# Graph network layer: features rotated and turned a batch ahead, radial units regrouped, axes summed on VectorE

## The reference

```
x = _layernorm(x + _L0_gnn_ref(x, src, dst), axis=-1)
x = _layernorm(x + _L1_gnn_ref(x, edge_weight, edge_attr_3, edge_index, w1, b1, w2, b2), axis=-1)
...
R = jax.nn.relu(abs_distances[:, None] @ w1 + b1) @ w2 + b2
Y = spherical_harmonics(rel_vec)
Fj = features[src]
...
            acc = acc + _NORM[i] * jnp.einsum('euv,ef,evi,ofi->euo', Rb[..., k], Yf, Fb, C)
...
out = out.at[dst].add(msg)
```

## Time and profile before

| | us |
|---|---|
| median of 3 runs (lowest, highest) | 3802.49 (3800.13, 3803.61) |
| the profiled execution | 3798.03 |
| its span | 3796.3 |
| TensorE busy | 3310.6 (87%) |
| GpSimd busy | 2786.3 (73%) |
| VectorE busy | 2762.8 (73%) |
| ScalarE busy | 2061.5 (54%) |

### The profile page before, as it was taken

The page is one execution under the profiler, slowest core; times in us unless marked ns, Lnnn a source line. Parts: engine busy times, 40 slices in busy tenths (PEclk is TensorE's granted clock), DMA queues, the critical chain, the costliest instruction groups (busy, mean ns, idle before and its releaser), DMA issues.

```text
span 3796.3 us, 58108 instructions
## 1 busy us (share of the span) xinstructions
PE 3310.6 (87%) x17312; PEld 1902.1 (50%) x17312; DVE 2762.8 (73%) x3470; ACT 2061.5 (54%) x2391; POOL 2786.3 (73%) x2915
## 2 busy tenths in 40 slices
PE   4999999999999883399999999999999999999963
PEld 3898889898989783222323232333323232323232
DVE  5787877787878785467777777777777777777765
ACT  4777777776777660145454545454554545454520
POOL 6777777777777776677777777777777777777746
PEclk9999999999999995599999999999999999999975
DMA  4122222222122211122222222222222222222211
GB/s 100 39 57 41 52 43 43 50 44 54 40 55 43 50 48 29 39 57 53 62 55 59 55 59 55 59 58 56 62 52 62 55 59 54 59 55 59 57 28 26
DMA packets 188428, 197.65 MB, mean 52 GB/s; under 512 B 60241, under 2 KB 149427, under 8 KB 188085
## 3 DMA queue, kind: packets, MB, share of 16 engines
q1 hardware_dynamic: 95508, 149.13, 13.7%
q0 software_dynamic: 92832, 47.72, 9.7%
HBM read 134.02 MB, written 62.59 MB: 52 GB/s over the span
## 4 chain that ended last, share of the span: by engine, by line
PE 70%; ACT 12%; DVE 5%; POOL 5%; issue 5%; DMA 1%; SPq 0%; ACTq 0%; DVEq 0%; POOLq 0%
PE ps_r L940 19%; PE ps_r L990 17%; PE ps_m L1027 10%; PE ps_m L940 10%; PE ps_r L1018 8%; ACT prod_room L822 8%; POOL ngot L667 4%; DVE unit L1645 3%; PE ps_m L1037 2%; PE ps_r L1002 2%; ACT f_across L829 2%; PE ps_r L924 1%; ACT hot_s L739 1%; PE ps_m L1043 1%; ACT hot_s L742 1%
## 5 line engine op out<-in xcount | busy, mean ns | idle before, releaser
L688 POOL DMA_INDIRECT got<-x_d,idx x1564 | 1506.2, 963 | 530.6 <-issue 504.7
L822 ACT ACTIVATE prod_room<-ps_r,bias_col 128x1024 f32<-128x1024 f32 x392 | 435.9, 1112 | 780.0 <-PE ps_r L990 531.9
L940 PE MATMUL ps_r<-x_hi,hot_s 128*128 128x448 f32 x1974 | 741.6, 376 | 41.7 <-ACT hot_s L742 41.7
L1645 DVE TENSOR_TENSOR x_room<-radial_more,ps_r 128x1024 f32<-128x1024 f32 x392 | 475.0, 1212 | 384.0 <-PE ps_r L1018 252.3
L990 PE MATMUL ps_r<-hid,wc 64*128 64x512 f32 (+1 forms) x2352 | 669.8, 646 | 81.2 <-ACT prod_room L822 72.9
L940 PE MATMUL ps_r<-x_lo,hot_s 128*128 128x448 f32 x1974 | 733.0, 371 | 0.0
L739 ACT ACTIVATE hot_s<-rows,minus_row 128x512 fp32r<-128x512 f16 (+1 forms) x658 | 449.0, 764 | 244.0 <-PE ps_m L940 206.2
L1018 PE MATMUL ps_r<-ft,repeat 32*128 32x512 f32 (+1 forms) x2352 | 553.4, 639 | 1.1 <-ACT ft L848 0.6
L1645 DVE TENSOR_TENSOR unit<-prod_room,ps_r 128x1024 f32<-128x1024 f32 x392 | 451.1, 1213 | 106.9 <-PE ps_r L1018 102.0
L940 PEld LDWEIGHTS ps_r<-x_hi,hot_s 128*128 128x128 f32 x1974 | 378.3, 192 | 75.5 <-issue 43.0
L990 PEld LDWEIGHTS ps_r<-hid,wc 64*128 64x128 f32 x2352 | 178.8, 186 | 448.8 <-ACT prod_room L822 255.3
(11 more groups left out here) (203 smaller groups left out, 4438.4 us busy)
## 6 DMA issues: line engine op xcount, KB each, us to landing
hid<-weight_t SPq DMA_DIRECT2D x196, 256.0 KB
run_d<-runs_t SPq DMA_DIRECT2D x194, 256.0 KB
got<-x_d,idx POOLq DMA_INDIRECT x1564
rows<-code_d SPq DMA_DIRECT2D x47, 160.0 KB
frame_d<-x_sb SPq DMA_DIRECT2D x7, 1008.0 KB, 4.5
frame<-frame_d SPq DMA_DIRECT2D x98, 72.0 KB
frame_b<-frame_d SPq DMA_DIRECT2D x98, 72.0 KB
rows<-code_d SPq DMA_DIRECT2D x47, 128.0 KB
```

Source lines behind the costliest of these rows:

```text
L688: pool.indirect_dma_start(got[k][:, t, :], None, x1_d, bass.IndirectOffsetOnAxis(ap=idx[k][:, t:t + 1], axis=0)).then_inc(got2_landed[k], 16)
L822: act.activation(radial_s[u][:, :, 0:w], radial_slot[:, :, 0:w], ACT.Identity, bias=bias_col[:, c:c + 1]).then_inc(radial_copied, 1)
L940: mm = pe.matmul(found[BANK_OF[k][g]], hot_s[k][:, a, g, :], part[:, a * LN * D:(a + 1) * LN * D], start=(a == 0 and n == 0), stop=(a == B ...
L1645: dve.tensor_tensor(product[q][h][:, :, 0:w], radial_s[u][:, :, 0:w], spread_slot[(k + s_ + 1) % 2][:, :, 0:w], ALU.mult).then_inc(multipl ...
```

## The change

Nothing of what is computed changes, and GpSimd's and SyncE's code stays as it is. In the message stage:

- Batch b + 1 is rotated in the body of batch b, between its multiplies 5 and 6, and turned, copied and given its index copy there. Transposed features get a bank of their own role (`turned_p`, the messages' bank), and `ft` two buffers, so the six spreads have both slots to themselves.
- Three radial units are made in the batch that uses them (3 to 5), three a batch ahead (0 to 2). The rectified weights (`relu`) are made one batch ahead rather than two.
- `add_axes` goes from TensorE. VectorE copies the scalars into `terms2` and adds the three axes with two instructions; `terms2` lies in SBUF now, so carry and scan read it there.

Some SBUF buffers of the input stage and the message stage share space differently; the order of the input stage doesn't change.

```diff
-STEPS = {"layer0": 8, "layer1": 16, "frames": 21}
+STEPS = {"layer0": 8, "layer1": 20, "frames": 21}
...
-ft = sb("ft", [P, QUAD * P])
+ft = [sb(f"ft{k}", [P, QUAD * P]) for k in range(2)]
...
-scalars_s = f_across[1][:, :, :, :, :].rearrange("p t a b v -> p (t a b v)")[:, 0:T * MUL].rearrange("p (t u) -> p t u", u=MUL)
+terms2 = f_across[1][:, :, :, :, :].rearrange("p t a b v -> p (t a b v)").rearrange("p (o t) -> p o t", t=T)
...
-terms2 = ps_m[:, 0, :].rearrange("p (o t) -> p o t", t=T)
+turned_p = ps_m[:, 0, :]
...
+def copy_turned(b, k, w=QUAD * P):
+
+    act.wait_ge(turned, b + 1)
+    if not isinstance(b, int) or b > 1:
+        act.wait_ge(spread_ready, UNITS * (b - 1))
+    act.copy(ft[k][:, 0:w], turned_p[:, 0:w]).then_inc(ft_ready, 1)
...
             masks2(b - 1, 1 - k)
+        copy_radial(b, 3, w)
+        copy_radial(b, 4, w)
         if not final:
-            later = TL // QUAD * P if last else QUAD * P
-            for u in range(4):
-                copy_radial(b + 1, u, later)
+            relu(1 - k, i + k + 1)
+        copy_radial(b, 5, w)
         if not first:
             carry_and_turn(b - 1, 1 - k)
-        if not last:
-            relu(k, i + 2)
         if not final:
-            copy_radial(b + 1, 4, later)
+            copy_radial(b + 1, 0, later)
+            copy_radial(b + 1, 1, later)
+            copy_scalars(b + 1, 1 - k, i + k, n)
+            if not last:
+                act.copy(idx[1 - k][:, :], src_all[:, bass.ds((b + 3) * T, T)]).then_inc(idx_ready, 1)
+            copy_turned(b + 1, 1 - k, later)
+            copy_radial(b + 1, 2, later)
...
-    if not isinstance(b, int) or b > 0:
-        pe.wait_ge(multiplied, len(PRODUCTS) * b - 1)
+    if not isinstance(b, int) or b > 1:
+        pe.wait_ge(back_ready, b - 1)
     for j in range(w // P):
-        mm = pe.transpose(spread_slot[k][:, 0, j * P:(j + 1) * P],
+        mm = pe.transpose(turned_p[:, j * P:(j + 1) * P],
...
-    slot = spread_slot[(k + s + 1) % 2]
+    slot = spread_slot[s % 2]
...
-        if not isinstance(b, int) or b > 0:
-            pe.wait_ge(multiplied, len(PRODUCTS) * b)
+    if s < 2 and (not isinstance(b, int) or b > 0):
+        pe.wait_ge(multiplied, len(PRODUCTS) * (b - 1) + s + 7)
...
-    if not isinstance(b, int) or b > 0:
-        pe.wait_ge(scanned, BATCHES + b)
+    pe.wait_ge(ft_ready, b + 1)
...
-def add_axes(b, n=T):
-    pe.wait_ge(back_ready, b + 1)
-    for a in range(3):
-        pe.matmul(terms2[:, MUL:D, :].rearrange("p (u i) t -> p t i u", i=3)[:, 0:n], ident[:, :],
-                  back[:, a, 0:n], start=(a == 0), stop=(a == 2), skip_group_check=True)
-    pe.matmul(terms2[:, 0:MUL, :].rearrange("p u t -> p t u")[:, 0:n], ident[:, :],
-              scalars_s[:, 0:n, :], start=False, stop=True, skip_group_check=True).then_inc(axes_summed, 1)
...
+        spread_features(b, k, 0, w)
         if not first:
             sum_products(b - 1, 3)
+        spread_features(b, k, 1, w)
+        if not first:
             turn_messages(b - 1)
-        turn_features(b, k, w)
+        radial(b, k, 3, w)
+        spread_features(b, k, 2, w)
+        radial(b, k, 4, w)
+        sum_products(b, 0, w)
+        radial(b, k, 5, w)
+        spread_features(b, k, 3, w)
+        sum_products(b, 1, w)
         if not final:
             radial(b + 1, 1 - k, 0, later)
-        spread_features(b, k, 0, w)
-        spread_features(b, k, 1, w)
-        if not first:
-            add_axes(b - 1)
+        spread_features(b, k, 4, w)
         if not final:
             radial(b + 1, 1 - k, 1, later)
-        spread_features(b, k, 2, w)
-        sum_products(b, 0, w)
-        sum_products(b, 1, w)
+        spread_features(b, k, 5, w)
         if not final:
             radial(b + 1, 1 - k, 2, later)
-        spread_features(b, k, 3, w)
-        if not final:
-            radial(b + 1, 1 - k, 3, later)
-        spread_features(b, k, 4, w)
-        if not final:
-            radial(b + 1, 1 - k, 4, later)
-        spread_features(b, k, 5, w)
+            turn_features(b + 1, 1 - k, later)
         sum_products(b, 2, w)
-        if not final:
-            radial(b + 1, 1 - k, 5, later)
...
-    s.mark(dve.tensor_copy(scalars_s[:, 0:n, :], messages[:, 0:n, 0:MUL]))
+    s.mark(dve.tensor_copy(terms2[:, 0:MUL, :].rearrange("p u t -> p t u")[:, 0:n], messages[:, 0:n, 0:MUL]))
...
     ins.then_inc(back_ready, 1)
+    s.settle()
+    s.mark(dve.tensor_tensor(back[:, 0, 0:n], back[:, 0, 0:n], back[:, 1, 0:n], ALU.add))
+    s.settle()
+    dve.wait_ge(back_ready, b + 1)
+    s.mark(dve.tensor_tensor(terms2[:, MUL:D, :].rearrange("p (u i) t -> p t i u", i=3)[:, 0:n],
+                             back[:, 0, 0:n], back[:, 2, 0:n], ALU.add))
...
-    dve.wait_ge(axes_summed, b + 1)
     dve.wait_ge(masks2_ready, b + 1)
+    s.settle()
...
+def rotate(b, k, rounds, n=T):
+
...
+        multiply(b, k, 0, w)
+        multiply(b, k, 1, w)
+        if begun:
             turn_back(b - 1, 1 - k)
-        for m in range(4):
-            multiply(b, k, m, w)
-        if not (first and k == 0):
+        multiply(b, k, 2, w)
+        multiply(b, k, 3, w)
+        multiply(b, k, 4, w)
+        if begun:
             scan2(b - 1, 1 - k)
-        for m in range(4, len(PRODUCTS)):
-            multiply(b, k, m, w)
-
+        multiply(b, k, 5, w)
+        if not final:
+            rotate(b + 1, 1 - k, i + k, TL if last else T)
+        multiply(b, k, 6, w)
+        multiply(b, k, 7, w)
+
+rotate(0, 0, 0)
```

More of the change, by code:

```diff
@@ L834, in layer1 @@
                     first, final = isinstance(b, int) and b == 0, last and k == 1
-                    n = TL if final else T
-                    w = TL // QUAD * P if final else QUAD * P
+                    n = TL if last else T
+                    w = (TL if final else T) // QUAD * P
+                    later = n // QUAD * P
                     if not first:
                         copy_summed(b - 1)
-                    act.wait_ge(got2_landed[k], 16 * (T * i + n))
-                    if not isinstance(b, int) or b > 1:
-                        act.wait_ge(turned, b - 1)
@@ L862, in _ @@
             act.wait_ge(loaded_net, 96)
             relu(0, 1)
-            relu(1, 1)
             act.wait_ge(bias_ready, 1)
-            for u in range(UNITS - 1):
+            for u in range(3):
                 copy_radial(0, u)
+            copy_scalars(0, 0, 0, T)
+            act.copy(idx[0][:, :], src_all[:, 2 * T:3 * T]).then_inc(idx_ready, 1)
+            copy_turned(0, 0)
             layer1(0)
@@ L1087, in _ @@
             mm.then_inc(bias_turned, 1)
-            for u in range(UNITS):
+            for u in range(3):
                 radial(0, 0, u)
@@ L1091, in _ @@
             pe.wait_ge(spreads_made, 1)
+            turn_features(0, 0)
             layer1(0)
@@ L1644, in multiply @@
                     dve.wait_ge(summed, BLOCKS * (b - 1) + q + 1)
-                dve.tensor_tensor(product[q][h][:, :, 0:w], radial_s[u][:, :, 0:w], spread_slot[(k + s_ + 1) % 2][:, :, 0:w],
+                dve.tensor_tensor(product[q][h][:, :, 0:w], radial_s[u][:, :, 0:w], spread_slot[s_ % 2][:, :, 0:w],
                                   ALU.mult).then_inc(multiplied, 1)
+            def rotate(b, k, rounds, n=T):
+                dve.wait_ge(got2_landed[k], 16 * (T * rounds + n))
+                dve.wait_ge(frame_loaded[k], 16 * (rounds + 1))
+                f1 = got[k][:, 0:n, MUL:D].rearrange("p t (v c) -> p t v c", c=3)
+                for c in range(3):
+                    s.mark(dve.tensor_tensor(part[:, c, 0:n], spread(f1[:, :, :, c], 2, 3),
+                                             spread(frame[k][:, 0:n, c, :], 3, MUL), ALU.mult))
+                s.settle()
+                s.mark(dve.tensor_tensor(part[:, 0, 0:n], part[:, 0, 0:n], part[:, 1, 0:n], ALU.add))
+                s.settle()
+                if not isinstance(b, int) or b > 1:
+                    dve.wait_ge(turned, b - 1)
+                dve.tensor_tensor(turned_in[k][:, 0:n, MUL:D], part[:, 0, 0:n].rearrange("p t i v -> p t (i v)"),
+                                  part[:, 2, 0:n].rearrange("p t i v -> p t (i v)"), ALU.add).then_inc(rotated_in, 1)
             def layer1(i, first, last=False):
```

46 lines of the change are left out of this document (13 added, 33 removed).

## The result

The changed kernel takes 3822.21 us (median of 5 runs, 3817.95 to 3825.92), the kernel before 3802.39 in the same comparison (3800.13 to 3803.61). The ratio is 1.0053 with a 95% interval of 1.0038 to 1.0068: slower by half a percent, and by more than the 0.2% that can be told from no change. The profiled execution spans 3820.5 us, 24.2 more than the 3796.3 of the one before.

The account below looks back on a forecast made before the run. The prediction took TensorE's loop as the bound, GpSimd's gathers 1% behind and binding after the change. Terms 44 - 10 - 19 + 2.5 = +17 us on 3798.0, with 4.5 to the median, gave 3820; range 3768 to 3868.

Parts of the forecast that it names:

- The bound: Message stage: GpSimd's 16 gathers a batch, 20.7 us, take over from the loop's 20.91; TensorE busy about 86% at full clock.
- The new waits: GpSimd issues held up by the scan and two additions now reading two SBUF tensors: 0.45 us a batch, +44 us.
- the measured share: Rotation's holds on GpSimd issues: 0.46 us a batch by the mean, 0.29 measured, so 0.64 of it.
- The rule behind it: About 0.15 us after its start, a GpSimd issue needs something VectorE holds while reading two SBUF tensors, then runs 0.79 us.
- The estimate h x h / 2.5: Mean wait of GpSimd issues, one every 1.25 us, for an instruction holding h; scan: h = 1.07, 0.46 us.
- the rival of nothing new: Nothing new holds GpSimd up, scans falling where no issue needs it: -27 us, 3776, chance 0.27.
- a full hit: GpSimd issues meet the scan at its front in every batch: +63 us, 3866, chance 0.14.
- The waits for the batch before the last: GpSimd's idle before a batch's first issue goes, since features are rotated a batch ahead: -10 us.
- The pauses: GpSimd's pause at the second issue of every seventh batch, about 36 us in 13 rows: taken as unchanged.
- The tail: Last issue to node stage: last rotation starts 2.4 us after the issue's end, -19 us; work after it +2.5 us.
- The loop's own turn: Message loop's work per batch without waiting for gathers: VectorE's path 17.3 us, TensorE 18.1 us, both under 20.0.
- The loop that stays slower: Message loop still slower than the gathers, TensorE queuing on VectorE's multiplies: at 21.5 us a batch +57, 3860; chance 0.07.

Follow-up runs that it names:

- e1b: Changed kernel, both additions still reading two SBUF tensors, only the second one's result put in PSUM for scan and carry: 3790.6 us, ratio 0.9980.
- e8: Changed kernel with SyncE's loads of the hidden weights, and the frames and store queued behind them, started one radial unit later: 3813.8 us, ratio 1.0042.
- e7: e1 with its first addition replaced by a copy into PSUM and an addition there: 3768.4 us, ratio 0.9909.
- e9: e1 with SyncE's loads of the hidden weights started one radial unit later: 3769.9 us, ratio 0.9925.
- e3p: e1 plus one unneeded VectorE instruction per batch, 1024 columns, one input from PSUM and one from SBUF: 4053.46 us, ratio 1.0658.
- e1: Changed kernel with the terms of scan and carry in PSUM again, the second addition also with a PSUM input: 3789.3 us, ratio 0.9973.
- e4: Changed kernel with the axes summed on TensorE as before, pipelining and radial order kept: 3829.0 us, ratio 1.0079.
- e6: Kernel before, not pipelined, with nothing but the axes moved to VectorE, summed into PSUM: 4144.8 us, ratio 1.0899.
- e3s: e1 plus one unneeded VectorE instruction per batch, 1024 columns, both inputs in SBUF: 4104.08 us, ratio 1.0803.
- e3c: e1 plus one unneeded VectorE instruction per batch, 1024 columns, reading one SBUF tensor and writing SBUF: 3803.39 us.
- e2b: Kernel before with 14 instead of 16 gathers in each batch from the third on: 3804.84 us, ratio 1.0004.

## Why the prediction was right

The bound and the cause were right; that 3820 lies only 2 us from 3822 is in part luck. The terms sum to +17 us, and the profiled spans differ by +24.2. The stream of gathers came out as the sum has it (+34, measured +33.7), but only because its waits were 4 us smaller and its pauses 5 us longer; the two ends, -16.5 by the sum, brought -9.5. The sum adds 4.5 us from the profiled execution to the median, and these did not come: the execution profiled after is itself the median.

- **The bound.** As predicted, the gathers became the bound: no wait for other engines, VectorE waiting at the rotation. Showing it took the two runs with 14 gathers. One sign missed: TensorE was not at 86% and the full clock but at 89% and 0.96.
- **The new waits**, +44 us. Measured 68.7 - 28.4 = +40.3 us. The scan has 23.9, or 0.25 a batch, a little under the measured share of its mean (0.64 x 0.46 = 0.29); the additions have 18.2 and not 0.13 x 97 = 13, since the second one, priced 0.56 to 0.59 us by the rotation's, takes 0.82 in the changed kernel, and 0.57 when it writes PSUM (e1b).
- **The rule behind it** needed mending. An instruction with two SBUF inputs does not hold an issue by running 0.15 us into it: it must have begun before the issue did. All 45 held scans had begun 0.31 to 0.67 us earlier; those that began from 0.03 us before an issue's start to 0.1 us after it held nothing. So the scan of the earlier trace rows, which began with its issue, could not have told whether scans hold; the 63 above can. The estimate h x h / 2.5 spread the scans evenly over a step. In truth they stood in two phases, about half of them at an issue's start or just behind it: the rival of nothing new and the rival of a full hit, half and half. That the mean came out near is luck of the phases; in e8 the same scans met 69 issues and cost 33.2 us.
- **The waits for the batch before the last**, -10 us: right. The gathers' idle time put down to ScalarE was 17.1 us, the usual gap of 0.305 of each row included; no row has more than that gap now.
- **The pauses**, taken as unchanged: +5 us, and as e7 and e9 show, they could have moved by 20. The prediction did not ask what sets their length, and it priced the shift of SyncE's loads, which e8 and e9 find behind it, at nothing.
- **The tail**, -19 + 2.5 us: -10.9. The last rotation did not follow the landing by 2.4 us. It began 6.2 us after the last issue, because VectorE first had a multiply, the carry, the scan and another multiply to do; from there to the node stage it took 28.8 us, 4.4 more than before and not 2.5.
- **The loop's own turn**, 17.3 and 18.1 us by two sums: 19.62 by the run with 14 gathers. This is the worst miss of the working. It did no harm since the gathers need more; but under a GpSimd without the new waits the margin is 1.2 us and not 2.6 (20.7 - 18.1), and in e3p an instruction of 1.2 us a batch on VectorE made the loop the bound again.
- **The rivals.** e1 makes the first one true, since nothing of the scan is held there: 3789 us, where 3776 was predicted; its first addition (8.8 us) and its pauses (8.1 more than before) come to more than that difference, and less beside the rotation (21.0 for 28.4) takes part of it back. The loop that stays slower came true only in variants: e4, e6, e3s and e3p.

## What to carry over

When another engine's queue of issues stands 1% behind the bound, price a change by what it does to that queue. Here a shortening of the loop by 1.3 us a batch (20.87 to 19.62) could not show, and where the scan's terms lay was worth 28 us in all. Before moving an operand from PSUM to SBUF on VectorE, look at which GpSimd issues run beside it; and with GpSimd as the bound, look at what its pauses coincide with.

## What was not expected of the hardware

- Which VectorE instructions hold up an issue of GpSimd: those with two SBUF inputs, wherever they write (e1's first addition writes PSUM and had 36 longer issues beside it), and the fast one of e3c with one SBUF input and SBUF output. Not held: PSUM and SBUF in (0 of 94), nor a copy from SBUF to PSUM (0 of 21 in e7). The Trainium skill, SBUF — State Buffer, section Who interferes with whom, says that tensor_scalar can enter a mode that takes the shared pair, and that whoever issues first keeps it for the whole instruction. The 79 held issues of e3c agree with the first. The scans that began with an issue or after it and held nothing agree with the second. The 13 issues of e3c that had begun before the fast instruction, and were longer all the same, do not.
- A VectorE instruction of 1.2 us per batch cost 2.35 us per batch (23.15 in e3p, 20.80 in e1). TensorE then waited more, and its granted clock over 1700 to 3500 us fell from 0.98 to 0.89; how the cost divides between the two was not separated. Window of e3p:

```profile
1700.00:3500.00 1800.00, 1582.86 (x6802) 424.92 (x6800) 1372.54 (x1780) 823.10 (x1004) 1202.30 (x1245) 0.89 0.22 52
```

- GpSimd's gathers pause by the count of issues, at every 112th: every 7th batch of 16, every 8th of 14. Where the gathers run on without waits, the start of SyncE's loads decides in nearly all of them whether a pause takes 2 us or 4: e1 had 12 pauses of 3.0 us and more, e9 with the loads moved has one. After a wait for the loop (e2b, e6) the same loads lengthen none.
